# Merging a layer norm with a mixture of experts, and spreading the routing weights by DMA

## The chip, the cores and the metric

The kernel runs on one core of a Trainium2 chip. Its time is the device time of one execution, in microseconds (us). Five engines work side by side and meet at semaphores: TensorE (PE, matrix products into PSUM banks of 128 x 512 float32), VectorE (DVE), ScalarE (ACT), GpSimd (POOL) and SyncE (SP), whose queue issues the transfers here. Everything below is float32 unless a row says bf16.

## The reference, cut to what matters

The input x has 4 sequences of 1024 tokens with 128 features, 4096 tokens in all. Four blocks follow one another, each added to x:

```python
x = x + delta_attention(layernorm(x))
x = x + ffn(layernorm(x))          # first mixture
x = x + decay_attention(layernorm(x))
x = x + ffn(layernorm(x))          # second mixture, same weights
```

The change lies in the two feed-forward mixtures and the plain layer norms before them:

```python
def layernorm(x, eps=1e-05):       # over the 128 features
    m, v = mean(x), var(x)
    return (x - m) / sqrt(v + eps)

def ffn(xt):                       # 15 experts, 3 of them per token
    shared = relu(xt @ sW1 + sb1) @ sW2 + sb2
    probs  = softmax(xt @ router_W + router_b)
    top_p, top_i = top_k(probs, 3)
    cw     = zeros((n, 15)); cw[row, top_i] = top_p
    h      = relu(einsum('nd,edh->neh', xt, eW1) + eb1)   # hidden size 128
    ye     = einsum('neh,ehd->ned', h, eW2) + eb2
    return shared + einsum('ned,ne->nd', ye, cw)
```

Every expert is computed for every token; the routing weight cw is zero for the twelve that were not chosen.

## The kernel before, in words

Activations stay in SBUF transposed: features on the 128 partitions, tokens along the row (g.xT, and g.xn for the normed copy). Work goes in NT = 8 tiles of 512 tokens. The kernel is a row of blocks; between two blocks all engines meet at a barrier and the semaphores of the block are cleared. Inside a block each engine has its own program, written in the order in which it runs, with explicit waits. There is no planner.

**The layer norm** (layernorm, L170 to L263). For each tile TensorE centres the features with a product (L191), ScalarE squares and copies the result (L224, L227), TensorE sums the squares (L198), ScalarE takes the square root (L233), VectorE inverts it (L246), TensorE spreads it over the partitions (L206), and VectorE multiplies (L253). The order of TensorE is variance(i), centre(i + 2), replicate(i - 1).

**The mixture** (mixture, L1248 to L1492). First a block b0 in which POOL raises about 80 semaphores by two (L1290). Then the main block: after a few memsets on VectorE, SP issues eleven loads (L1320), among them both sets of expert weights and a selecting matrix sel, and all engines wait for all of them. VectorE casts sel to bf16 (L1418). Then the routing of tile 0 runs alone: logits (r_lt, L1331 and L1385), their turn to tokens on partitions (r_tr, L1337), maximum and subtraction (r_sub), exponential (L1389), the three largest probabilities (r_top, L1427 to L1449), the turn back (r_ct, L1343), and a split of the weights into three bf16 parts that sum to the float32 value (r_parts, L1451 to L1466).

Then, for each tile, sixteen experts (the shared one is the sixteenth). For expert e TensorE computes the hidden layer ph (L1356) and the product pc that copies row e of the routing weights to all 128 partitions (L1358: sel times the three parts); ScalarE applies relu (L1399); VectorE multiplies by pc (L1478, a plain copy L1480 for the shared expert) into hs; TensorE adds the second layer into py (L1367). ph, pc, hr and hs have two buffers each, and TensorE runs hidden(e + 1) before the second layer of e. The bias product (L1363) opens py. The routing of the next tile is laid between the experts: r_lt behind e = 1, r_tr behind e = 3, r_ct behind e = 10 on TensorE, r_top behind e = 6 and r_parts behind e = 11 on VectorE. At the end of a tile VectorE adds py to x (L1490). The tile loop is a hardware loop over pairs of tiles with two tiles behind it (tiles, L1304).

Of the kernel before, what the change touches and what calls it, by code (L numbers as in the profile page):

```python
# [31 lines left out]
CREDIT = 2  # L32
TILE = 512
# [8 lines left out]


def done(n):

    return n + 1 + CREDIT


def constants():
# [1198 lines left out]
def mixture(nc, g, tag):  # L1248


    NE = E_N + 1
    with ExitStack() as ctx:
        new_sem = semaphores(nc, ctx)
        sb = lambda n, s, dt=F32: ctx.enter_context(nc.sbuf_tensor(tag + n, s, dt))
        pb = lambda n, s: ctx.enter_context(nc.psum_tensor(tag + n, s, F32))
        sem = lambda n: new_sem(tag + n)
        w1, w2 = sb("w1", [128, NE, 128]), sb("w2", [128, NE, 128])
# [6 lines left out]
        mx = sb("mx", [128, 4])  # L1264
        den = sb("den", [128, 4])
        p20 = sb("p20", [128, 4, 20])
        m20 = sb("m20", [128, 4, 20])
# [4 lines left out]
        rest = sb("rest", [NE, 2, TILE])  # L1272
        midw = sb("midw", [NE, TILE], BF16)
        parts = [sb(f"parts{i}", [96, TILE], BF16) for i in range(2)]
        hr, hs = sb("hr", [128, 2, TILE]), sb("hs", [128, 2, TILE])
        ph, pc, py = ([pb(f"{n}{i}", [128, TILE]) for i in range(2)] for n in ("ph", "pc", "py"))
        pl, pt = pb("pl", [128, TILE]), pb("pt", [128, TILE])
        evs = []

        def ev(n):  # L1280
            evs.append(sem(n))
            return evs[-1]

        hc_mm, relu, hs_ev, y_mm = ([ev(f"{n}{e}") for e in range(NE)] for n in ("hc_mm", "relu", "scaled", "y_mm"))
        lt_mm, lt_ev, tr_mm, mx_ev, sub_ev, exp_ev, den_ev, rden_ev, p_ev, top_ev, topf_ev, m_ev, cw_ev, ct_mm, ct_ev = (
            ev(n) for n in ("lt_mm", "lt_ready", "tr_mm", "max_ready", "sub_ready", "exp_ready", "den_ready", "rden_ready", "p_ready",
                            "top_ready", "top3_ready", "match_ready", "cw_ready", "ct_mm", "cwt_ready"))
        hi_ev, r1_ev, mid_ev, r2_ev, parts_ev, acc_ev = (ev(n) for n in ("hi_ready", "r1_ready", "mid_ready", "r2_ready", "parts_ready", "acc_ready"))
        loaded, zeroed, const = sem("loaded"), sem("zeroed"), sem("const")
        with nc.Block() as b0:  # L1290
            @b0.gpsimd
            def _(pool):
                for s in evs:
                    pool.sem_inc(s, CREDIT)
        block = ctx.enter_context(nc.Block())
        d = g.dram
        loads = [(w1[:, 0:E_N, :], d["eW1"].rearrange("e d h -> d e h")), (w1[:, E_N, :], d["sW1"]),
                 (w2[:, 0:E_N, :], d["eW2"].rearrange("e d h -> d e h")), (w2[:, E_N, :], d["sW2"]),
                 (b1[:, 0:E_N], d["eb1"].rearrange("e h -> h e")), (b1[:, E_N:NE], d["sb1"].unsqueeze(1)),
                 (b2[0:E_N, :], d["eb2"]), (b2[E_N:NE, :], d["sb2"].unsqueeze(0)),  # L1300
                 (rw[:, 0:E_N], d["router_W"]), (rb[0:E_N, :], d["router_b"].unsqueeze(1)), (self32[:, :], d["c_sel"])]
        NPAIR = NT // 2

        def tiles(eng, step, lead):  # L1304

            lead(0, 0, 0)
            with eng.Fori(0, NPAIR - 1) as j:
# [511 lines left out]
```

## Time and profile before

| what | us |
|---|---|
| median of three runs (3720.75 to 3724.38) | 3722.41 |
| the profiled execution's own time | 3720.53 |
| its span, first to last instruction | 3718.7 |
| first merged stretch: first centring product of the norm to the end of the mixture's last addition | 2556.59 to 2924.13 |
| second one | 3337.67 to 3705.70 |

Busy shares over the whole span are PE 90%, PEld (weight loads) 68%, DVE 75%, ACT 61% and POOL 56%, but most of the span is the delta attention (up to 2554.96), which has nothing to do with the change. A span is what the instructions cover; the execution's own time adds what lies around it, 1.8 us here. All times of rows are us from the start of the span. A reader should look at the stretches of the norms and mixtures alone. One float32 product over 512 columns shows as two MATMUL records; the durations of overlapping records are modelled, so the distance between the starts tells more than the duration.

### The profile page before, as it was taken

How to read it: one execution, taken by the hardware profiler on the slowest of the kernel's cores; microseconds unless marked ns; L12 is line 12 of the kernel's file. 1: busy time of each engine (PE TensorE's matmuls, PEld its weight loads, DVE VectorE, ACT ScalarE, POOL GpSimd, SP SyncE). 2: the span in 40 equal slices, each digit the busy share in tenths (PEclk: the TensorE clock that was granted, in tenths of full speed). 3: DMA queues.
4: the chain of work that ended last, by engine and by line, in shares of the span. 5: the costliest groups of instructions: out<-in, count | busy, mean ns of one | idle time of the engine just before them, and what ended most of it. 6: DMA issues, size and time to landing. Idle time of an engine off the chain costs nothing. (4 is left out here: it accounts for less than half of the span.)

```text
span 3718.7 us, 84350 instructions
## 1 busy us (share of the span) xinstructions
PE 3337.8 (90%) x27220; PEld 2546.1 (68%) x27220; DVE 2786.4 (75%) x6092; ACT 2254.8 (61%) x6799; POOL 2067.5 (56%) x3164
## 2 busy tenths in 40 slices
PE   5359999999999999999999999996899876795998
PEld 3248888888888888888888888874333456672333
DVE  3469999999999999999999999763444469543443
ACT  3368888888888888888888888742233310002333
POOL 1188888888888888888888888830000027100000
PEclk8679999999999999999999999998899985557999
DMA  2557787788787778778877777632000000001000
GB/s 63 160 132 180 181 180 166 175 188 177 170 182 173 178 179 174 171 171 187 179 170 179 171 174 180 159 95 56 1 0 0 1 10 1 1 1 31 0 0 23
DMA packets 603120, 429.38 MB, mean 115 GB/s; under 512 B 497164, under 2 KB 524332, under 8 KB 602700
## 3 DMA queue, kind: packets, MB, share of 16 engines
q1 hardware_dynamic: 600396, 417.86, 49.4%
q10 hardware_dynamic: 2304, 6.29, 0.6%
q8 instruction: 218, 3.57, 0.5%
q14 instruction: 202, 1.65, 0.2%
HBM read 224.25 MB, written 199.75 MB: 114 GB/s over the span
## 5 line engine op out<-in xcount | busy, mean ns | idle before, releaser
L743 POOL TENSOR_TENSOR X<-X,tmp 96x31 f32<-96x31 f32 (+15 forms) x992 | 534.1, 538 | 77.8
L740 POOL TENSOR_TENSOR tmp<-At,X 96x31 f32<-96x31 f32 (+15 forms) x992 | 482.4, 486 | 118.8 <-DMA At<-n_d 63.6
L1610 POOL TENSOR_TENSOR b_P<-b_P,b_tmp 128x512 f32<-128x512 f32 x80 | 114.4, 1430 | 517.6 <-DVE b_tmp L1628 512.8
L1101 PE MATMUL PP<-xn,wk 128*128 128x268 f32 x1024 | 310.9, 406 | 61.3 <-DMA tk<-in_conv_q_dram 41.0
L708 POOL TENSOR_TENSOR Sg<-S,gend 128x512 f32<-128x512 f32 x256 | 276.4, 1080 | 109.8 <-DVE S L927 109.8
L803 ACT ACTIVATE conv_k<-PP,tk 128x256 f32<-128x256 f32 x512 | 235.9, 471 | 108.0 <-PE PP L1101 102.5
L1065 PE MATMUL RB<-rhs,Yf 96*96 96x128 f32 x2048 | 276.3, 278 | 9.8 <-DVE rhs L916 9.3
L767 ACT ACTIVATE recA<-TG 128x128 f32<-128x128 f32 x1024 | 265.6, 275 | 31.8 <-PE TG L1152 31.8
L1065 PEld LDWEIGHTS RB<-rhs,Yf 96*96 96x96 f32 x2048 | 239.6, 163 | 64.7 <-DVE rhs L916 52.5
L775 ACT ACTIVATE recA<-TG,es 96x128 f32<-96x128 f32 x1024 | 273.7, 368 | 16.2 <-DVE es L951 15.9
L1055 PE MATMUL RA<-S,kqgB 128*96 128x128 f32 x2048 | 275.1, 277 | 0.7 <-DVE S L927 0.7
L1075 PE MATMUL RA<-ws,recB 96*128 96x128 f32 x2048 | 271.5, 276 | 0.7 <-ACT ws L793 0.7
L1055 PEld LDWEIGHTS RA<-S,kqgB 128*96 128x96 f32 x2048 | 240.2, 163 | 39.8 <-issue 25.2
L1075 PEld LDWEIGHTS RA<-ws,recB 96*128 96x128 f32 x2048 | 260.0, 192 | 7.7 <-ACT ws L793 0.9
L965 DVE SCALAR_TENSOR_TENSOR conv_k<-PP,tk,conv_k 128x256 f32<-128x256 f32 x512 | 247.8, 484 | 18.3
L963 DVE SCALAR_TENSOR_TENSOR conv_k<-PP,tk,conv_k 128x256 f32<-128x256 f32 x512 | 247.7, 484 | 18.2
L961 DVE SCALAR_TENSOR_TENSOR conv_k<-PP,tk,conv_k 128x256 f32<-128x256 f32 x512 | 244.2, 477 | 22.2 <-ACT conv_k L803 20.6
L803 ACT ACTIVATE conv_v<-PP,tv 128x256 f32<-128x256 f32 x384 | 183.7, 478 | 126.7 <-PE PP L1101 112.3
L693 POOL TENSOR_TENSOR kqgA<-kq,gdec 128x768 f32<-128x768 f32 x128 | 202.7, 1584 | 80.4 <-ACT kq L844 73.6
L1101 PE MATMUL PP<-xn,wv 128*128 128x268 f32 x768 | 242.1, 396 | 2.1 <-DVE conv_k L965 2.1
L1101 PEld LDWEIGHTS PP<-xn,wk 128*128 128x128 f32 x1024 | 170.8, 197 | 82.2 <-DMA tk<-in_conv_q_dram 41.8
L1164 PE MATMUL TG<-kq 128*96 128x128 f32 x1888 | 225.6, 273 | 0.7 <-ACT recA L775 0.7
(314 smaller groups left out, 8396.6 us busy)
## 6 DMA issues: line engine op xcount, KB each, us to landing
kqg_d<-kqgA SPq DMA_DIRECT2D x128, 512.0 KB, 5.1
kqgB<-kqg_d SPq DMA_DIRECT2D x128, 512.0 KB, 7.3
rec_d<-recA SPq DMA_DIRECT2D x128, 480.0 KB, 3.7
recB<-rec_d SPq DMA_DIRECT2D x128, 480.0 KB, 8.6
gdec<-gdec_d SPq DMA_DIRECT2D x128, 128.0 KB, 6.6
apk_d<-apkA SPq DMA_DIRECT2D x128, 128.0 KB, 2.5
apkB<-apk_d SPq DMA_DIRECT2D x128, 128.0 KB, 6.7
edec<-edec_d SPq DMA_DIRECT2D x128, 96.0 KB, 6.2
```

Of the source, the lines that this page charges most:

```text
L708: nc.gpsimd.tensor_tensor(Sg[:, :, :], S[cc][:, :, :], d.broadcast_to([128, B, 128]), ALU.mult).then_inc(sg_ev[cc], 1)
L740: nc.gpsimd.tensor_tensor(t, At[q % 2][:, j, j + 1:].unsqueeze(2).broadcast_to(sh), X[q % 2][:, j, 0:cols].unsqueeze(1).broadcast_to(sh), ...
L743: nc.gpsimd.tensor_tensor(x, x, t, ALU.subtract).then_inc(sub_ev, 1)
L767: last = nc.scalar.activation(recA[N % 2][:, u * 128:(u + 1) * 128], TG[:, u, :], ACT.Square, accum_out=ksum[:, u:u + 1])
L775: last = nc.scalar.activation(recA[N % 2][0:R, u * 128:(u + 1) * 128], TG[0:R, u, :], ACT.Copy, scale=es[:, u, TC - 1:TC])
L803: nc.scalar.activation(acc, src[:, :, 0:SPAN], ACT.Copy, scale=w).then_inc(tap0_ev[i], 1)
L963: nc.vector.scalar_tensor_tensor(acc, src[:, :, 2:2 + SPAN], w[:, 2:3], acc, ALU.mult, ALU.add).then_inc(t2_ev[i], 1)
L965: nc.vector.scalar_tensor_tensor(acc, src[:, :, 3:3 + SPAN], w[:, 3:4], acc, ALU.mult, ALU.add).then_inc(taps_ev[i], 1)
L1055: last = mm(RA[0:R, b, :], kqgB[N % 2][:, b * NCC + cc, 0:R], S[cc][:, b, :], start=True, stop=True)
L1065: last = mm(RB[0:R, b, :], Yf[N % 2][:, b * NCC + cc, :], rhs[:, b, :], start=True, stop=True)
L1075: last = mm(RA[:, b, :], recB[N % 2][:, u * 128:(u + 1) * 128], ws[cc][:, b, :], start=True, stop=True)
L1101: mm(out, w, x, start=True, stop=True).then_inc(tile_mm[i], 1)
```

## The change

The norm and the mixture behind it become one function and one block, twice. The weights are issued by SP at the block's start, in the order router, first layer, second layer, with a semaphore for each group, while the norm runs. The routing of tile 0 is laid into the norm's loop. The block of POOL increments is gone, and the tile loop is written out. The three bf16 parts, sel and the product pc are gone. In their place VectorE copies the routing weights of a tile to cwt (r_cwt), SP stores the 15 rows of cwt to DRAM, waits for that, and issues four transfers that read 4, 4, 4 and 3 rows back into all 128 partitions (gates, 15 x 512 float32 on each partition, two buffers). VectorE then multiplies hr by gates, both in SBUF. ph, hr and hs have four buffers, TensorE runs hidden(e + 2) before the second layer of e, also over the tile's end, and the addition to x moves behind the second expert of the next tile. In the routing of the next tile r_lt, r_tr and r_ct stand behind e = 0, 2 and 7, and VectorE's r_sub, r_top and r_cwt behind e = 3, 5 and 8. The functions take, root, centre, variance, replicate, invert and norm are those of layernorm; r_sub and r_top are the same instructions as before.

```diff
-    sel = np.zeros((96, E_N, 128), np.float32)
-    for part in range(3):
-        for e in range(E_N):
-            sel[32 * part + e, e] = 1
-    c["c_sel"] = sel.reshape(96, -1)
...
-def mixture(nc, g, tag):
-
+def normed_mixture(nc, g, tag):
 
     NE = E_N + 1
+    QUARTER = TILE // 4
+    DEEP = 4
+    GROUPS = [(0, 4), (4, 8), (8, 12), (12, E_N)]
...
-        self32 = sb("sel32", [96, E_N * 128])
-        sel = sb("sel", [96, E_N, 128], BF16)
+        xc = sb("xc", [128, 4, TILE])
+        sq = sb("sq", [128, 2, TILE])
+        rs = sb("rs", [128, 4, QUARTER])
+        eps = sb("eps", [128, 1])
...
+        gates = [sb(f"gates{i}", [128, E_N, TILE]) for i in range(2)]
+        hr, hs = sb("hr", [128, DEEP, TILE]), sb("hs", [128, DEEP, TILE])
+        gates_d = nc.dram_tensor(tag + "gates_d", (2, E_N, TILE), F32, kind="Internal").ap()
+        ph = [pb(f"ph{i}") for i in range(DEEP)]
+        py = [pb(f"py{i}") for i in range(2)]
+        pl, pt = pb("pl"), pb("pt")
+        cen, var, rep = ph[0:2], ph[2:4], py
...
         @block.sync
         def _(sp):
             sp.wait_ge(zeroed, 1)
...
-            for dst, src in loads:
-                sp.dma_start(dst, src, allow_slow_non_contiguous=True).then_inc(loaded, 16)
+            sp.dma_start(rw[:, 0:E_N], d["router_W"], allow_slow_non_contiguous=True).then_inc(router_in, 16)
+            sp.dma_start(rb[0:E_N, :], d["router_b"].unsqueeze(1), allow_slow_non_contiguous=True).then_inc(router_in, 16)
+            sp.dma_start(w1[:, 0:E_N, :], d["eW1"].rearrange("e d h -> d e h")).then_inc(w1_in, 16)
...
+            for n in range(NT):
+                sp.wait_ge(ct_ev, n + 1)
+                sp.dma_start(gates_d[n % 2], cwt[n % 2][0:E_N, :]).then_inc(gates_out, 16)
+                sp.wait_ge(gates_out, 16 * (n + 1))
+                need(sp, hs_ev[E_N - 1], n - 2)
+                for k, (a, b) in enumerate(GROUPS):
+                    sp.dma_start(gates[n % 2][:, a:b, :], gates_d[n % 2, a:b].partition_broadcast(128)).then_inc(gates_in[n % 2][k], 16)
...
+            def r_lt(n):
+                if n == 0:
+                    pe.wait_ge(router_in, 32)
+                    pe.wait_ge(scaled, 1)
+                need(pe, ct_ev, n - 1)
+                mm(pl[0:NE, :], rw[:, :], xn_of(n), start=True, stop=True).then_inc(lt_mm, 1)
...
+            def hidden(n, e):
+                n, e = n + e // NE, e % NE
+                if n == NT:
+                    return
+                if e >= DEEP:
+                    pe.wait_ge(relu[e - DEEP], n + 1)
+                else:
+                    need(pe, relu[NE + e - DEEP], n - 1)
+                mm(ph[e % DEEP][:, :], w1[:, e, :], xn_of(n), start=True, stop=True).then_inc(h_mm[e], 1)
+
+            centre(0)
+            centre(1)
+            for i in range(NT + 1):
+                if i < NT:
+                    variance(i)
+                if i + 2 < NT:
+                    centre(i + 2)
+                if i:
+                    replicate(i - 1)
+                if i == 2:
+                    r_lt(0)
+                if i == 4:
+                    r_tr(0)
+                if i == 7:
+                    r_ct(0)
+            pe.wait_ge(scaled, NT)
+            pe.wait_ge(copied, NT)
+            pe.wait_ge(rooted, NT)
+            pe.wait_ge(w1_in, 64)
+            hidden(0, 0)
+            hidden(0, 1)
+            pe.wait_ge(w2_in, 64)
+            for n in range(NT):
+                pe.wait_ge(ct_ev, n + 1)
+                need(pe, acc_ev, n - 2)
+                mm(py[n % 2][:, :], b2[:, :], cwt[n % 2][:, :], start=True, stop=False)
                 for e in range(NE):
...
+                    hidden(n, e + 2)
+                    pe.wait_ge(hs_ev[e], n + 1)
+                    mm(py[n % 2][:, :], w2[:, e, :], hs[:, e % DEEP, :], start=False, stop=e == NE - 1).then_inc(y_mm[e], 1)
+                    if n + 1 < NT:
+                        if e == 0:
+                            r_lt(n + 1)
+                        if e == 2:
+                            r_tr(n + 1)
+                        if e == 7:
+                            r_ct(n + 1)
...
+            act.wait_ge(eps_ready, 1)
+            take(0)
+            take(1)
+            for i in range(NT):
+                root(i)
+                if i + 2 < NT:
+                    take(i + 2)
+                if i == 2:
+                    act.wait_ge(router_in, 32)
+                    r_lt(0)
+                if i == 5:
+                    r_exp(0)
+            act.wait_ge(w1_in, 64)
+            for n in range(NT):
                 for e in range(NE):
-                    act.wait_ge(hc_mm[e], done(n))
-                    act.wait_ge(hs_ev[e - 2], done(n) if e >= 2 else done(n - 1))
-                    nc.scalar.activation(hr[:, e % 2, :], ph[e % 2][:, :], ACT.Relu, bias=b1[:, e:e + 1]).then_inc(relu[e], 1)
-                    if n1 is not None:
+                    act.wait_ge(h_mm[e], n + 1)
+                    if e >= DEEP:
+                        act.wait_ge(hs_ev[e - DEEP], n + 1)
+                    else:
+                        need(act, hs_ev[NE + e - DEEP], n - 1)
+                    nc.scalar.activation(hr[:, e % DEEP, :], ph[e % DEEP][:, :], ACT.Relu, bias=b1[:, e:e + 1]).then_inc(relu[e], 1)
+                    if n + 1 < NT:
                         if e == 2:
-                            r_lt(n1)
-                        if e == 5:
-                            r_exp(n1)
-
-            tiles(act, step, lead)
+                            r_lt(n + 1)
+                        if e == 4:
+                            r_exp(n + 1)
...
+            def r_cwt(n):
+                dve.wait_ge(ct_mm, n + 1)
+                need(dve, y_mm[0], n - 2)
+                if n >= 2:
+                    dve.wait_ge(gates_out, 16 * (n - 1))
+                nc.vector.tensor_copy(cwt[n % 2][:, :], pl[0:NE, :]).then_inc(ct_ev, 1)
...
+            invert(0)
+            for i in range(NT):
+                if i + 1 < NT:
+                    invert(i + 1)
+                norm(i)
+                if i == 3:
+                    r_sub(0)
+                if i == 5:
+                    r_top(0)
+            def add(n):
+                dve.wait_ge(y_mm[NE - 1], n + 1)
+                nc.vector.tensor_tensor(x_of(n), py[n % 2][:, :], x_of(n), ALU.add).then_inc(acc_ev, 1)
+
+            r_cwt(0)
+            for n in range(NT):
                 for e in range(NE):
-                    dve.wait_ge(relu[e], done(n))
-                    dve.wait_ge(y_mm[e - 2], done(n) if e >= 2 else done(n - 1))
+                    if n and e == 2:
+                        add(n - 1)
+                    dve.wait_ge(relu[e], n + 1)
+                    if e >= DEEP:
+                        dve.wait_ge(y_mm[e - DEEP], n + 1)
+                    else:
+                        need(dve, y_mm[NE + e - DEEP], n - 1)
                     if e < E_N:
-                        nc.vector.tensor_tensor(hs[:, e % 2, :], pc[e % 2][:, :], hr[:, e % 2, :], ALU.mult).then_inc(hs_ev[e], 1)
+                        if e % 4 == 0:
+                            dve.wait_ge(gates_in[n % 2][e // 4], 16 * (n // 2 + 1))
+                        nc.vector.tensor_tensor(hs[:, e % DEEP, :], gates[n % 2][:, e, :], hr[:, e % DEEP, :], ALU.mult).then_inc(hs_ev[e], 1)
                     else:
-                        nc.vector.tensor_copy(hs[:, e % 2, :], hr[:, e % 2, :]).then_inc(hs_ev[e], 1)
-                    if n1 is not None:
-                        if e == 4:
-                            r_sub(n1)
-                        if e == 6:
-                            r_top(n1)
-                        if e == 11:
-                            r_parts(n1, 1 - par)
-                dve.wait_ge(y_mm[NE - 1], done(n))
-                x = g.xT[:, bass.ds(j, 1), TILE * par:TILE * (par + 1)]
-                nc.vector.tensor_tensor(x, py[par][:, :].unsqueeze(1), x, ALU.add).then_inc(acc_ev, 1)
-
-            tiles(dve, step, lead)
+                        nc.vector.tensor_copy(hs[:, e % DEEP, :], hr[:, e % DEEP, :]).then_inc(hs_ev[e], 1)
+                    if n + 1 < NT:
+                        if e == 3:
+                            r_sub(n + 1)
+                        if e == 5:
+                            r_top(n + 1)
+                        if e == 8:
+                            r_cwt(n + 1)
+            add(NT - 1)
...
-        layernorm(nc, g, "ln1", x_tile)
-        mixture(nc, g, "f1")
+        normed_mixture(nc, g, "f1")
...
-        layernorm(nc, g, "ln4", x_tile)
-        mixture(nc, g, "f2")
+        normed_mixture(nc, g, "f2")
```

## Rows read from the trace of the kernel before

**Rows 1.** Busy time by engine in both mixtures: us, PE, PEld, DVE, ACT, POOL, PEclk, DMA, GB/s

```profile
2618.65:2924.13 305.48, 287.24 (x746) 117.69 (x746) 132.77 (x332) 93.67 (x142) 0.00 (x0) 0.98 0.00 0
3400.24:3705.70 305.46, 287.23 (x746) 117.82 (x746) 132.77 (x332) 93.67 (x142) 0.00 (x0) 0.98 0.00 0
```

**Rows 2.** Groups of instructions, first mixture: busy, mean ns | idle before, releasers

```profile
L1367 PE MATMUL f1py<-f1hs,f1w 128*128 128x512 f32 x256 | 134.4, 606 | 17.5 <-DVE f1hs L1478 14.9 <-DVE f1hs L1480 2.6
...
L1478 DVE TENSOR_TENSOR f1hs<-f1pc,f1hr 128x512 f32<-128x512 f32 x120 | 82.3, 691 | 148.3 <-ACT f1hr L1399 148.0
```

**Rows 3.** Timeline of one undisturbed expert: start, us, engine, line, op, count

```profile
2910.33 1.02 PE L1356 MATMUL f1ph<-xn,f1w 128*128 128x512 f32 x2
...
2911.19 0.38 PE L1358 MATMUL f1pc<-f1parts,f1sel 96*128 96x512 bf16 x1
...
2911.41 1.02 PE L1367 MATMUL f1py<-f1hs,f1w 128*128 128x512 f32 x2
...
2912.27 1.02 PE L1356 MATMUL f1ph<-xn,f1w 128*128 128x512 f32 x2
```

**Rows 4.** Timeline of one whole tile, from fifteenth expert to fifteenth expert

```profile
2735.80 1.07 PE L1367 MATMUL f1py<-f1hs,f1w 128*128 128x512 f32 x2
...
2744.46 1.03 PE L1331 MATMUL f1pl<-xn,f1rw 128*16 x2
...
2749.49 1.06 PE L1337 MATMUL f1pt<-ident,f1lt 16*128 16x16 f32 x8
...
2750.48 1.12 PE L1356 MATMUL f1ph<-xn,f1w 128*128 x2
...
2764.82 0.60 PE L1343 MATMUL f1pl<-ident,f1cw 128*16 128x128 f32 x4
...
2773.91 1.07 PE L1367 MATMUL f1py<-f1hs,f1w 128*128 128x512 f32 x2
```

**Rows 5.** Timeline of norm, lead-in and end of the first mixture

```profile
2556.59 3.75 PE L191 MATMUL ln1cen<-xT,centre 128*128 128x512 f32 x4 [2.08 <-PEq L91]
...
2579.01 0.69 DVE L253 TENSOR_TENSOR xn<-ln1rep,ln1xc 128x512 f32<-128x512 f32 x1 [0.70 <-PE ln1rep L206]
...
2604.35 1.16 DVE L1418 CAST f1sel<-f1sel 96x1920 bf16<-96x1920 f32 x1 [16.12 <-DMA f1sel<-in_c_sel_dram]
...
2625.38 1.92 PE L1367 MATMUL f1py<-f1hs,f1w 128*128 128x512 f32 x2
...
2923.44 0.69 DVE L1490 TENSOR_TENSOR xT<-f1py,xT 128x512 f32<-128x512 f32 x1 [1.22 <-PE f1py L1367]
```

**Rows 6.** Timeline of VectorE, first and last instruction of r_top

```profile
2755.13 0.20 DVE L1429 TENSOR_REDUCE f1den<-f1lg 128x4 f32<-128x60 f32 x1
...
2757.17 0.22 DVE L1449 SCALAR_TENSOR_TENSOR f1cw<-f1m,f1p 128x60 f32<-128x60 f32 x1
```

**Rows 7.** Timeline of ScalarE in the norm, table load and square root

```profile
2561.48 1.28 ACT L233 ACT_TABLE_LOAD   x1
...
2562.77 0.37 ACT L233 ACTIVATE ln1rs<-ln1var,ln1eps 128x128 f32<-128x128 f32 x1
```

**Rows 8.** DMA issues of the whole span: KB each, median us to landing

```profile
gdec<-gdec_d SPq DMA_DIRECT2D x128, 128.0 KB, 6.6
...
apkB<-apk_d SPq DMA_DIRECT2D x128, 128.0 KB, 6.7
...
n_d<-apkA SPq DMA_DIRECT2D x384, 32.0 KB, 2.2
...
xin<-in_x_dram SPq DMA_DIRECT2D x4, 512.0 KB, 4.0
```

**Rows 9.** Busy time by engine: the loads at their densest, and the delta attention

```profile
2592.00:2594.00 2.00, 0.00 (x0) 0.00 (x0) 0.00 (x0) 0.00 (x0) 0.00 (x0) 0.50 1.17 297
...
600.00:700.00 100.00, 99.84 (x1007) 85.84 (x1006) 94.54 (x215) 85.58 (x280) 85.00 (x135) 1.00 0.83 188
```

**Rows 10.** Busy time by engine: TensorE's clock as it rises, norm and mixture

```profile
2561.00:2562.00 1.00, 1.00 (x7) 0.24 (x9) 0.00 (x0) 0.98 (x2) 0.00 (x0) 1.00 0.00 0
...
2628.00:2630.00 2.00, 2.00 (x5) 0.57 (x3) 0.00 (x0) 0.69 (x1) 0.00 (x0) 0.76 0.00 0
```

More of the change, by code:

```diff
@@ L1295, in mixture @@
+        zeroed, router_in, w1_in, w2_in, gates_out = (sem(n) for n in ("zeroed", "router_in", "w1_in", "w2_in", "gates_out"))
+        gates_in = [[sem(f"gates_in{p}_{k}") for k in range(len(GROUPS))] for p in range(2)]
         block = ctx.enter_context(nc.Block())
         d = g.dram
[L1297 to L1307, printed above, removed]
-                step(j * 2, j, 0, j * 2 + 1, j)
-                step(j * 2 + 1, j, 1, j * 2 + 2, j + 1)
-            step(NT - 2, NPAIR - 1, 0, NT - 1, NPAIR - 1)
-            step(NT - 1, NPAIR - 1, 1, None, None)
-        def xn(j, par):
-            return g.xn[:, bass.ds(j, 1), PAD + TILE * par:PAD + TILE * (par + 1)]
+        x_of = lambda i: g.xT[:, i // 2, TILE * (i % 2):TILE * (i % 2 + 1)]
@@ L1340, in r_ct @@
             def r_ct(n):
[L1341 removed]
+                pe.wait_ge(cw_ev, n + 1)
                 for a in range(4):
@@ L1376, in _ @@
-            tiles(pe, step, lead)
+            def hidden(n, e):
[22 more added lines that the diff above has]
+                    r_ct(0)
@@ L1378, in _, with take, root @@
         @block.scalar
         def _(act):
-            act.wait_ge(loaded, 16 * len(loads))
+            def take(i):
+                act.wait_ge(centred, i + 1)
+                need(act, varied, i - 2)
+                nc.scalar.activation(sq[:, i % 2, :], cen[i % 2][:, :], ACT.Square).then_inc(squared, 1)
+                need(act, scaled, i - 4)
+                nc.scalar.activation(xc[:, i % 4, :], cen[i % 2][:, :], ACT.Copy).then_inc(copied, 1)
+            def root(i):
+                act.wait_ge(varied, i + 1)
+                need(act, spread, i - 4)
+                nc.scalar.activation(rs[:, i % 4, :], var[i % 2][:, 0:QUARTER], ACT.Sqrt, bias=eps[:, :]).then_inc(rooted, 1)
@@ L1451, in r_parts @@
-            def r_parts(n, par):
-                dve.wait_ge(ct_mm, done(n))
-                dve.wait_ge(y_mm[NE - 1], done(n - 2))
-                hi, mid, lo = (parts[par][32 * i:32 * i + NE, :] for i in range(3))
-                nc.vector.tensor_copy(cwt[par][:, :], pl[0:NE, :]).then_inc(ct_ev, 1)
-                nc.vector.tensor_copy(hi, pl[0:NE, :]).then_inc(hi_ev, 1)
-                dve.wait_ge(hi_ev, done(n))
-                nc.vector.tensor_tensor(rest[:, 0, :], pl[0:NE, :], hi, ALU.subtract).then_inc(r1_ev, 1)
-                dve.wait_ge(r1_ev, done(n))
-                nc.vector.tensor_copy(midw[:, :], rest[:, 0, :]).then_inc(mid_ev, 1)
-                dve.wait_ge(mid_ev, done(n))
-                nc.vector.tensor_copy(mid, midw[:, :])
-                nc.vector.tensor_tensor(rest[:, 1, :], rest[:, 0, :], midw[:, :], ALU.subtract).then_inc(r2_ev, 1)
-                dve.wait_ge(r2_ev, done(n))
-                nc.vector.tensor_copy(lo, rest[:, 1, :]).then_inc(parts_ev, 1)
@@ L1468, in lead @@
-            def lead(n, j, par):
-                r_sub(n)
-                r_top(n)
-                r_parts(n, par)
-            def step(n, j, par, n1, j1):
-                for e in range(NE):
-                    dve.wait_ge(relu[e], done(n))
-                    dve.wait_ge(y_mm[e - 2], done(n) if e >= 2 else done(n - 1))
+            invert(0)
[7 more added lines that the diff above has]
+                    r_top(0)
```

180 lines of the change are left out of this document (75 added, 105 removed).

## The prediction

> **What bounds the kernel now.** I read the busy time by stage first. Each mixture's main part lasts 305.5 us with TensorE busy 287, VectorE 133, ScalarE 94 and no DMA [rows 1]. So TensorE sets the pace there, and the DMA engines are free. The groups by line then say what TensorE still waits for: 17.5 us of idle time before the second-layer product L1367, released by VectorE [rows 2].
>
> The timeline of one expert gives the price list: hidden product 0.86 us (start to start, less the copy product), copy product 0.22, second layer 0.86, together 1.94 [rows 3]. Any float32 product over 512 columns costs 0.86. A whole tile takes 2773.91 - 2735.80 = 38.1 us [rows 4]. Its work is 15 x 1.94 + 1.72 = 30.8 for the experts, 0.86 for the bias product, 0.86 for the logits, 0.99 for r_tr (2749.49 to 2750.48) and 0.60 for r_ct, in all 34.1. The other 4.0 us are waits: two buffers leave little room when VectorE is away for r_top (2755.13 to 2757.39 = 2.26 us [rows 6]) or for the seven instructions of r_parts.
>
> The timeline of the lead-in shows the second cost. The norm ends at 2579.01 + 0.69 = 2579.70, VectorE gets its last load and casts sel at 2604.35 after waiting 16.1 us for transfers, and the first second-layer product starts at 2625.38 [rows 5]. From the block's start to that product pass 68.8 us, of which the norm is 23.1.
>
> **The change, part by part.** Times are for one mixture; the second has the same main part to 0.02 us [rows 1], and I take it as equal.
>
> *Norm with the routing of tile 0 inside.* TensorE gets r_lt and r_tr before the norm's end, 0.86 + 0.99 = 1.85, and is fully busy there [rows 10]. ScalarE must change tables for the exponential between two square roots and back: two loads of 1.28 [rows 7] and the small exponential, 2.8. VectorE has r_top, 2.26, in front of invert(7), and the norm's tail is a chain through all three engines. The three add up to 6.9 if nothing overlaps. Bounds: 3 (all but the table change hidden) and 9. I take 6.9, since the tail is serial: the norm ends at +30.0.
>
> A rule of the Trainium skill speaks against this step (ScalarE: Activation LUTs, What ACT_TABLE_LOAD costs): a switch costs the load and a drain of about 1.38 us more. In rows 7 the square root starts 1.29 us after its load does, so this trace shows no drain; by the rule the two switches would add 2.8 us a mixture, and the forecast would be 5.5 us later.
>
> *Loads.* Their wait (16.1 us, rows 5) lies under a norm of 30 us; without c_sel there is less of it. SP issues nothing else then. Cost nothing; if the cover were gone, at most the few us by which they end later than the norm.
>
> *From the norm's end to the first expert.* r_cwt is one copy, 0.7. The store is 30 KB; the nearest row has 32 KB landing in 2.2 [rows 8]. SP waits for it and issues the four broadcasts; behind that wait on SP stand only these. The first moves 128 x 8 KB = 960 KB. The nearest plain load is 512 KB in 4.0 [rows 8]; the other 448 KB at 297 GB/s [rows 9] make 1.5, together 5.5. From below the pure rate bounds it, 983,040 bytes at 297 = 3.3; from above the only broadcast in the trace, 128 KB in 6.6 among other traffic [rows 8], and the rest at 188 GB/s [rows 9], 11.1. Then one multiplication, 0.7, and hand-overs of 0.2: 30.0 + 0.7 + 2.2 + 5.5 + 0.9 = +39.3. Before it was +68.8, so 29.5 us go. By then three hidden products and the bias product are done.
>
> *The tile.* No pc: 15 x 0.22 = 3.3 us less. The waits: between the end of hidden(e) and the second layer of e now lie four products, 3.4 us. Relu 0.69, multiplication 0.69 [rows 2] and three hand-overs take about 1.7. VectorE's r_top behind e = 5 takes 2.26; the next multiplication ends 2.26 + 0.69 = 2.95 after the last, and is due 1.7 + 1.72 = 3.4 after it: hidden. r_cwt is short. At the tile's end the hidden products run on. So all 4.0 us go; bounds 0 and 4.0. What is late next is TensorE itself: 32 x 0.86 + 0.86 + 0.86 + 0.99 + 0.60 = 30.8 with routing, 28.4 in the last tile. VectorE has about 16 us of work in it. The multiplication from two SBUF operands has no row; it could take up to 2.4 us (0.69 + the 1.7 of room) without being seen.
>
> *The gates of the next tile.* From r_ct to the next tile's first second layer TensorE has 18 products, 15.5 us; less cwt 0.9 and one multiplication 0.7, 13.9 remain for store and first broadcast, 7.7. The other groups come every 3.3 us and are used up in 4 x 1.72 = 6.9. All four are 3.93 MB: 13.2 us at 297 GB/s, 20.9 at 188, both under 30.8. Hidden. Uncovered, the tile would last as long as its transfers; that begins under 128 GB/s. TensorE and VectorE lose nothing to traffic by rows 9: TensorE is 99.84% busy at full clock beside 188 GB/s.
>
> *The clock.* TensorE stands idle for some us before the first gates and starts at 1.2 GHz (0.50). In the norm the full clock (1.00) is there 4 to 5 us after the first product, in the mixture it comes about 11 us after 2618.65 [rows 1, 10]. Half speed over 7 us, between them, loses 3.5; bounds 0 and 5.5.
>
> *The sum.* From the first second layer: 7 x 30.8 + 28.4 - 4 x 0.86 = 240.6, + 3.5 for the clock, + 0.9 for the last addition = 245.0. Before: 2924.13 - 2625.38 = 298.8. So 53.8 + 29.5 = 83.3 a mixture, 166.5 in both. The profiled execution took 3720.53: 3554.0. It lies 1.9 under the median shown, so 3556.
>
> **The rivals.**
>
> *A: stalls stay.* Waits move to the gates' semaphores or to VectorE. For: VectorE waits in order and r_top is within 0.5 us of the limit. Against: 1.7 us of room each expert. If all 4.0 stay in 16 tiles: 3556 + 64 = 3620.
>
> *B: the broadcasts set the pace, but the kernel is still faster.* 128 partitions read the same 8 KB at once, from few places in DRAM. Against: the broadcast in rows 8 lands as fast as a plain load of its size, 6.6 against 6.7. For: that is an eighth of the size and bound by latency. At 110 GB/s the tile is 35.7: + 4.9 x 16 = 78, 3634; anywhere from 3560 to 3715.
>
> *C: slower than before.* The same mechanism below a threshold: the saving of 166 us is eaten when a tile takes 166 / 16 = 10.4 us more, 41.2, that is below 95 GB/s. Its form: a transfer that runs on a quarter of the 16 DMA engines, 297 / 4 = 74 GB/s, tile 53, + 22 x 16 = 355: 3910. For: groups have four rows. Against: rows 8, and every load onto 128 partitions in rows 9 runs near 300.
>
> The Trainium skill (DMA: Bandwidth & Descriptors, Rules for kernel authors) has the rule behind C: the slowest dimension of both sides sets how many engines a DMA uses, so a leading broadcast of few copies confines it to as many. Here the leading dimension is the 128 partitions, which by the rule uses all 16; no run here shows it for this shape yet.
>
> *D: the change doesn't do what it says.* The loads might not end under the norm: they took 16 us alone, and now start with it. Then the lead-in keeps up to 10 us, + 20: 3576. The trace gives nothing for that.
>
> **How the numbers follow.** Forecast 0.76, A 0.09, B 0.08, C 0.05, D 0.02. The forecast's own range adds its bounds: from -(3.9 norm, 2.2 first gates, 3.5 clock) x 2 = -19 to +(2.1 + 5.6 + 2.0) x 2 = +19, 3537 to 3575. Up to 3620 it takes in A, D and part of B: 3535 to 3620, with about 2 in 10 outside, most of it below my trust in the small terms. About 0.2% (7 us) is what a measurement of this kernel can tell from no change. Faster 0.94, same 0.01 (B or C close to 95 GB/s), slower 0.05.
>
> **What would show it.** Right: no MATMUL from sel; starts of second-layer products 1.72 apart, r_top included; tiles of 30.8 with TensorE busy throughout; first second layer about 39 us after the first centring product, with 7 to 8 us of TensorE idle before it released by a DMA; transfers done 13 to 21 us after their issue in each tile. Wrong: VectorE waiting for gates in tiles 1 to 7 (B, C), idle time on TensorE behind r_top (A), ScalarE or TensorE waiting for w1 or w2 (D). A norm that ends before +27 or after +33 would make my 6.9 wrong.

## The result, and the profile after

The changed kernel takes 3561.21 us (median of 4 runs, 3555.57 to 3564.35), the kernel before beside it 3722.22: a ratio of 0.9566, 95% interval 0.9552 to 0.9581. The forecast was 3556, in a range of 3535 to 3620. In a second set of 5 runs (a1_after) it took 3558.09 against 3722.92, ratio 0.9558 [0.9545, 0.9571]; the experiments below are compared with this one. "Ratio" is the time over that of the kernel before in the same set, with its 95% interval.

The profiled execution took 3555.57, its span is 3553.5. The two merged stretches, busy time by engine, from the first centring product to the end of the last addition (columns as in [rows 1]):

```profile
2560.36:2847.12 286.76, 280.41 (x784) 122.83 (x784) 126.36 (x333) 111.63 (x172) 0.00 (x0) 0.96 0.31 118
3253.46:3540.01 286.55, 280.29 (x784) 123.03 (x784) 126.36 (x333) 111.63 (x172) 0.00 (x0) 0.96 0.31 119
```

TensorE is busy for 280.4 of 286.8 us. Before, the same stretch lasted 2924.13 - 2556.59 = 367.5 us [rows 5], so 80.8 us went here and about 81 in the second, 162 of the 165 between the two profiled runs. I had forecast 284.3 and 83.3.

The groups that answer to [rows 2], from the first second-layer product on:

```profile
L1386 PE MATMUL f1py<-f1hs,f1w 128*128 128x512 f32 x256 | 131.3, 595 | 0.0
L1355 PE MATMUL f1ph<-xn,f1w 128*128 128x512 f32 x251 | 131.0, 603 | 0.0
L1526 DVE TENSOR_TENSOR f1hs<-f1gates,f1hr 128x512 f32<-128x512 f32 x119 | 81.8, 690 | 100.7 <-ACT f1hr L1438 100.7
L1386 PEld LDWEIGHTS f1py<-f1hs,f1w 128*128 128x128 f32 x256 | 48.5, 190 | 62.4 <-issue 60.5 <-DVE f1hs L1526 1.4 <-DVE f1hs L1528 0.4
```

The 17.5 us in front of the second-layer product are 0.0 now, and from here on VectorE's multiplication waits for ScalarE's relu alone, never for gates. The last row is the weight load that belongs to the product, on an engine row of its own (PEld): its 1.4 us behind VectorE are idle time of the loads, not of the products. TensorE's timeline over one tile, from bias product to bias product (answers to [rows 4]):

```profile
2723.87 1.02 PE L1386 MATMUL f1py<-f1hs,f1w 128*128 128x512 f32 x2
2724.82 1.12 PE L1382 MATMUL f1py<-f1cwt,f1b 16*128 16x512 f32 x2
2725.87 1.13 PE L1355 MATMUL f1ph<-xn,f1w 128*128 128x512 f32 x2
2726.83 1.02 PE L1386 MATMUL f1py<-f1hs,f1w 128*128 128x512 f32 x2
2727.78 1.03 PE L1332 MATMUL f1pl<-xn,f1rw 128*16 128x512 f32 x2
2728.75 1.12 PE L1355 MATMUL f1ph<-xn,f1w 128*128 128x512 f32 x2
2729.71 1.02 PE L1386 MATMUL f1py<-f1hs,f1w 128*128 128x512 f32 x2
2730.57 1.02 PE L1355 MATMUL f1ph<-xn,f1w 128*128 128x512 f32 x2
2731.43 1.02 PE L1386 MATMUL f1py<-f1hs,f1w 128*128 128x512 f32 x2
...
2756.32 1.12 PE L1382 MATMUL f1py<-f1cwt,f1b 16*128 16x512 f32 x2
```

Second layers stand 2731.43 - 2729.71 = 1.72 apart, as forecast, but the tile is 2756.32 - 2724.82 = 31.50, not 30.8: around the bias product, the logits and r_tr, whose shapes differ, the starts stand 0.95 to 1.05 apart and not 0.86. TensorE waits for nothing; these 0.7 us are its own.

The norm's end and the lead-in, which answer to [rows 5]:

```profile
2580.47 1.28 ACT L1416 ACT_TABLE_LOAD   x1
2581.76 0.25 ACT L1416 ACTIVATE f1lg<-f1lg 128x60 f32<-128x60 f32 x1
2582.03 1.28 ACT L1407 ACT_TABLE_LOAD   x1
2583.33 0.62 ACT L1407 ACTIVATE f1rs<-f1ph,f1eps 128x128 f32<-128x128 f32 x2
2583.73 0.95 DVE L1449 RECIPROCAL f1rs<-f1rs 128x128 f32<-128x128 f32 x1 [2.78 <-ACT f1rs L1407]
...
2590.43 0.69 DVE L1454 TENSOR_TENSOR xn<-f1py,f1xc 128x512 f32<-128x512 f32 x1 [1.62 <-PE f1py L1324]
...
2591.73 0.32 SPq L1299 DMA_DIRECT2D f1gates_d<-f1cwt  x1
...
2593.26 2.03 SPq L1303 DMA_DIRECT2D f1gates<-f1gates_d  x4
...
2596.89 2.08 PE L1355 MATMUL f1ph<-xn,f1w 128*128 128x512 f32 x2
...
2598.06 1.29 DVE L1526 TENSOR_TENSOR f1hs<-f1gates,f1hr 128x512 f32<-128x512 f32 x2 [6.36 <-DMA f1gates<-f1gates_d]
...
2598.81 2.08 PE L1386 MATMUL f1py<-f1hs,f1w 128*128 128x512 f32 x2
```

The norm ends at 2591.12, +30.8 from the start (a time with a plus sign counts from the merged stretch's first centring product); the first second-layer product stands at +38.4, in the second mixture too. Broadcasts, as a DMA group of the page and by busy time (the last three columns are the granted clock, the DMA share and GB/s):

```profile
f1gates<-f1gates_d SPq DMA_DIRECT2D x24, 1024.0 KB, 6.6
```

```profile
2595.00:2597.00 2.00, 2.00 (x3) 0.50 (x3) 0.00 (x0) 0.68 (x1) 0.00 (x0) 0.50 1.03 426
2601.00:2603.00 2.00, 2.00 (x3) 0.37 (x2) 0.00 (x0) 0.26 (x1) 0.00 (x0) 0.54 0.97 410
2603.00:2605.00 2.00, 2.00 (x6) 0.80 (x6) 0.40 (x1) 1.10 (x2) 0.00 (x0) 1.00 0.57 229
2632.00:2847.00 215.00, 214.39 (x540) 91.94 (x538) 94.83 (x249) 81.19 (x122) 0.00 (x0) 1.00 0.27 111
```

They keep all 16 DMA engines busy (shares of 0.97 to 1.03) at 410 to 426 GB/s, over the 297 of [rows 9]; in the tiles they fill 27% of the time.

### The profile page after: what moved, and what is told of

Read it like the earlier page. It is cut to its first block and busy times, and to the rows that moved or that the text cites. A ratio compares the mean times of both kernels' runs of the same rounds, so it can differ in the third digit from the quotient of the medians.

```text
span 3553.5 us, 83210 instructions
## 1 busy us (share of the span) xinstructions
PE 3264.9 (92%) x26980; PEld 2519.4 (71%) x26980; DVE 2732.4 (77%) x5990; ACT 2264.8 (64%) x6803; POOL 2070.6 (58%) x3164
## 5 line engine op out<-in xcount | busy, mean ns | idle before, releaser
L1054 PEld LDWEIGHTS RB<-rhs,Yf 96*96 96x96 f32 x2048 | 239.5, 162 | 64.8 <-DVE rhs L905 52.5
L952 DVE SCALAR_TENSOR_TENSOR conv_k<-PP,tk,conv_k 128x256 f32<-128x256 f32 x512 | 247.8, 484 | 18.2
```

The lines of the kernel that those rows point to most:

```text
L952: nc.vector.scalar_tensor_tensor(acc, src[:, :, 2:2 + SPAN], w[:, 2:3], acc, ALU.mult, ALU.add).then_inc(t2_ev[i], 1)
L1054: last = mm(RB[0:R, b, :], Yf[N % 2][:, b * NCC + cc, :], rhs[:, b, :], start=True, stop=True)
```

## The experiments

**The whole change, and the merging alone.** a1_after is the changed kernel again.

> The changed kernel again, for its spread and for a second profile. If the changed parts are steady and the 9 us between its runs come from elsewhere (theory: TensorE's clock in the two attentions, which the change does not touch), both merged stretches last 286 to 287 us again, first centring product to last addition, and the rest of the span differs by several us from the first profile. If the spread comes from the broadcasts (rival), the merged stretches differ by several us between the profiles and VectorE waits for gates in some tile after the first.

Measured: 3558.09 (above). The theory holds: the merged stretches last 286.0 and 286.6 us, and the time between them is 9.6 us longer than in the first profile (415.9 for 406.3), in parts that the change does not touch. a2_merge merges norm and mixture and loads under the norm, but keeps the copy product with r_parts, the two buffers (the ring of two) and the old order in the tile:

Its edit against the changed kernel, the core of it:

```
-    DEEP = 4
+    DEEP = 2
...
+            sp.dma_start(self32[:, :], d["c_sel"]).then_inc(sel_in, 16)
...
-                    sp.dma_start(gates[n % 2][:, a:b, :], gates_d[n % 2, a:b].partition_broadcast(128)).then_inc(gates_in[n % 2][k], 16)
...
+                        last = mm(pc[e % 2][:, :], sel[:, e, :], parts[n % 2][:, :], start=True, stop=True)
...
-                    hidden(n, e + 2)
+                    hidden(n, e + 1)
...
-                        if e == 7:
+                        if e == 10:
                             r_ct(n + 1)
...
+                nc.vector.tensor_copy(hi, pl[0:NE, :]).then_inc(hi_ev, 1)
```

> Only the merging: norm and mixture in one block, loads under the norm, routing of tile 0 in the norm, no block of POOL increments, tile loop written out; but the copy product from three bf16 parts, two buffers, hidden(e + 1) and the old places of the routing stay. Theory: the first second-layer product comes at +43 us instead of +68.8 (norm to +30.8, seven instructions of r_parts 4.3, cast 1.2, five cold products 6.7) and the tiles stay at 38.1, so 3722 - 2 x 26 = 3670. Rival, that writing the loop out or the moved addition matters too: below 3655.

Measured: 3673.93 (3672.14 to 3675.03), ratio 0.9870 [0.9854, 0.9885]. First second-layer product at +42.7, tiles of 38.11 as before. Merging is worth 49 us, all of it ahead of the first expert: from the first second-layer product on, the two mixtures last 299.0 and 298.7 us, in the kernel before 298.8 and 298.7.

**The ring.** a3_ring2 is the changed kernel with two buffers instead of four:

```
-    DEEP = 4
+    DEEP = 2
...
-        cen, var, rep = ph[0:2], ph[2:4], py
+        var = [pb(f"var{i}") for i in range(2)]
+        cen, rep = ph, py
...
             hidden(0, 0)
-            hidden(0, 1)
...
-                    hidden(n, e + 2)
+                    hidden(n, e + 1)
```

> The changed kernel with rings of two for ph, hr and hs and hidden(e + 1) ahead of the second layer; gates by DMA as in the change. Between the end of hidden(e) and the second layer of e stand two products, 1.72 us, against 1.66 for relu, multiplication and hand-overs. Theory, the ring hides what VectorE does between: r_top 2.3, cwt 0.7, the addition 0.7 and the subtraction 0.5 come out on TensorE, about 4 us a tile, + 64: 3625. Rival, the waits of before came from the copy product and r_parts, which are gone anyway: within 15 us of the changed kernel, 3575.

Measured: 3582.65 (3573.93 to 3586.73), ratio 0.9623 [0.9603, 0.9644]; tiles of 32.85. My theory was wrong, the rival (3575) nearly right. TensorE in one tile of this kernel, around r_top:

```profile
2740.89 1.02 PE L1356 MATMUL f1ph<-xn,f1w 128*128 128x512 f32 x2
2742.72 1.13 PE L1386 MATMUL f1py<-f1hs,f1w 128*128 128x512 f32 x2 [0.80 <-DVE f1hs L1526]
2743.68 1.02 PE L1356 MATMUL f1ph<-xn,f1w 128*128 128x512 f32 x2
```

One wait a tile, 0.80 us with 0.17 of start-up, and nothing of the rest, but for slips of 0.05. The kernel before had three, of which two end here (lines of its timeline, same columns):

```profile
2757.25 0.38 PE L1358 MATMUL f1pc<-f1parts,f1sel 96*128 96x512 bf16 x1
2758.04 1.13 PE L1367 MATMUL f1py<-f1hs,f1w 128*128 128x512 f32 x2 [0.41 <-DVE f1hs L1478]
...
2768.05 0.38 PE L1358 MATMUL f1pc<-f1parts,f1sel 96*128 96x512 bf16 x1
2770.15 1.13 PE L1367 MATMUL f1py<-f1hs,f1w 128*128 128x512 f32 x2 [1.72 <-DVE f1hs L1478]
...
2775.31 1.13 PE L1367 MATMUL f1py<-f1hs,f1w 128*128 128x512 f32 x2 [0.33 <-DVE f1hs L1480]
```

0.22 is the undisturbed distance, so 0.57 is lost behind r_top and 1.88 behind r_parts. At the last expert 0.54 more is lost: its second layer starts at 2775.31, 1.40 behind the one at 2773.91 [rows 4], where 0.86 is undisturbed. The largest was r_parts, which went with the copy product, without a deeper ring.

So the gain is made up of 49.0 for merging, 3673.9 - 3582.7 = 91.3 for gates by DMA, and 3582.7 - 3558.1 = 24.6 for the ring; by the mixtures' own lengths in the traces it is 52.5, 86.0 and 23.8. The middle part is not the gates alone. a3_ring2 differs from a2_merge in the order of the tile too: the routing of the next tile stands earlier, the addition is moved, and the hidden products run on over the tile's end. The 0.54 us at the last expert went with that order, in 16 tiles about 9 us (an estimate). No run has four buffers together with the copy product, so what the ring alone would have given the old kernel stays open.

**The threshold of rival B.** a4_four issues three spare copies beside each broadcast, into tiles that nobody reads: 15.73 MB a tile instead of 3.93.

```
                     sp.dma_start(gates[n % 2][:, a:b, :], gates_d[n % 2, a:b].partition_broadcast(128)).then_inc(gates_in[n % 2][k], 16)
+                    for x in range(3):
+                        need(sp, spare_in[x], 16 * (4 * n + k) - 1)
+                        sp.dma_start(spare[x][:, 0:b - a, :], gates_d[n % 2, a:b].partition_broadcast(128)).then_inc(spare_in[x], 16)
```

> The changed kernel, but every broadcast is followed by three more of the same rows into spare buffers that nobody reads, so 15.7 MB a tile instead of 3.93. If the rate of 425 GB/s that the profile shows in one tile holds, a tile's transfers take 37.0 us and with the store between them about 40, more than TensorE's 30.8: tiles of 40, + 9.2 x 14 = + 129, about 3690, and VectorE waits for gates. If the rate falls under sustained load to the 297 that I had assumed, tiles of 55 and about 3900. If transfers cost TensorE or VectorE time of their own, products and multiplications show longer durations.

Measured: 3704.63 (3703.15 to 3707.73), ratio 0.9952 [0.9936, 0.9968]. Busy time over six tiles (the last three columns are again the granted clock, the DMA share and GB/s), and VectorE's group in them:

```profile
2640.00:2880.00 240.00, 207.57 (x482) 83.42 (x480) 81.44 (x234) 71.57 (x108) 0.00 (x0) 0.94 0.95 391
```

```profile
L1533 DVE TENSOR_TENSOR f1hs<-f1gates,f1hr 128x512 f32<-128x512 f32 x90 | 59.1, 686 | 131.0 <-DMA f1gates<-f1gates_d 103.7 <-ACT f1hr L1445 27.3
```

The wait in front of the multiplication is a DMA's now, as rival B has it. The tiles take 39.98 on average (bias products at 2639.43 and 2879.29, six tiles), and 15.73 MB in that are 393 GB/s. It takes four times the traffic to bring the kernel back near its old time, and even then VectorE's multiplication lasts 686 ns beside it, not more than the 690 of the changed kernel. The mixtures last 355.5 and 359.9, together 142.0 more than the changed kernel's. My 129 counted 14 tiles. From the first bias product to the last, 14 tiles of the two mixtures, 118.7 us were added; the two last tiles, from the bias product to the end of the last addition, take 38.8 and 40.1 us instead of 27.8, 23.3 more. They wait for their gates too, and I had left them out: most of the 14.6 us over my 3690.

**Loads not hidden (rival D).** c_late holds the weight loads until the norm is done:

```
             sp.dma_start(rb[0:E_N, :], d["router_b"].unsqueeze(1), allow_slow_non_contiguous=True).then_inc(router_in, 16)
+            sp.wait_ge(scaled, NT)
             sp.dma_start(w1[:, 0:E_N, :], d["eW1"].rearrange("e d h -> d e h")).then_inc(w1_in, 16)
```

> The changed kernel with the mixture's weight loads held back until the norm's last product. Theory: placing them under the norm is worth what they take behind it: SP needs about 9.6 us to issue them and the last lands 6 us later, so the store of the gates comes 9 to 10 us later and the first second-layer product at about +50 instead of +38.5: 3558 + 23 = 3581. Rival: the routing and the gates' trip would have covered most of it anyway: 3558 + 6 = 3564.

Measured: 3579.34 (3573.91 to 3582.82), ratio 0.9611 [0.9596, 0.9627]; first second-layer product at +48.0 and +47.8, each mixture 296.8, 10.1 more. In the timeline of SP's queue the store of the gates stands behind the eight issues:

```profile
2588.24 0.41 SPq L1290 DMA_DIRECT2D f1w<-in_eW_dram  x1
...
2590.49 3.32 SPq L1293 DMA_DIRECT2D f1b<-in_sb_dram  x1
...
2596.67 0.32 SPq L1300 DMA_DIRECT2D f1gates_d<-f1cwt  x1
...
2600.21 1.96 SPq L1304 DMA_DIRECT2D f1gates<-f1gates_d  x4
```

The delay is first SP's issuing, 2596.67 - 2588.24 = 8.4 us, then a store that takes 3.5 instead of 1.5 us to come back. In the changed kernel, where the loads start is worth 21 us in all. That it is also 21 of the 49 us of merging is not shown: a2_merge was not run with late loads.

**The norm's tail.** b1_exp_late moves tile 0's exponential behind the last root, so that no table is loaded back:

```
-                if i == 7:
+                if i == NT:
                     r_ct(0)
...
-                if i == 5:
-                    r_exp(0)
+            r_exp(0)
...
-                if i == 5:
+                if i == 6:
                     r_top(0)
```

> The changed kernel with the exponential of tile 0 behind the last square root, r_top(0) behind the seventh norm product and r_ct(0) behind the last replication. Theory: the norm's tail waits for the two table loads (VectorE idle 2.8 us before the seventh reciprocal) and with the exponential last, one of the two leaves the path and r_top fills another engine's time: the norm ends 4 us earlier (at +26.5 to +27), the first second-layer product at +34.5; 3558 - 8 = 3550. Rival: the tail is set by the router's own chain (exponential, r_top, r_ct, cwt) wherever it stands: within 2 us of 3558.

Measured: 3552.71 (3547.24 to 3565.22), ratio 0.9552 [0.9534, 0.9570]. The times overlap with those of a1_after, the traces decide: the norm ends at +26.6 in both mixtures (before the move +30.8), the first second-layer product is at +34.2 and +34.4, the mixtures last 282.8 and 283.0. The theory holds: the reload and r_top in front of the last reciprocal, moved together here, cost 4.2 us of the tail; no run parts the two.

b2_small_first splits off the first gate row:

```
-    GROUPS = [(0, 4), (4, 8), (8, 12), (12, E_N)]
+    GROUPS = [(0, 1), (1, 4), (4, 8), (8, 12), (12, E_N)]
```

> The changed kernel with broadcasts of 1, 3, 4, 4 and 3 gate rows instead of 4, 4, 4 and 3. Theory: the first multiplication waits for 1 MB at about 420 GB/s, and would be released some 1.9 us earlier by a quarter of it; TensorE, which waits for the gates for only 1.4 us, gains 1 us a mixture at most: 3556. Rival: the landing is latency, not bytes, and nothing changes: 3558. In the tiles neither sees a difference, since the gates are there early.

Measured: 3560.17 (3544.96 to 3562.74), ratio 0.9565 [0.9551, 0.9578]: medians cannot tell 2 us here. The first multiplication starts at +36.8 in both mixtures, 0.4 to 0.9 us earlier than in the two profiles of the changed kernel, not 1.9. A first group of 256 KB lands 3.8 us after its issue, one of 1024 KB after 4.2 to 4.7, so the landing is mostly latency. But this run's two mixtures, the same instructions, lasted 283.9 and 286.5. Busy time at about equal distance from their starts (+34.7 and +35.0):

```profile
2589.00:2591.00 2.00, 2.00 (x4) 0.48 (x4) 0.00 (x0) 0.64 (x1) 0.00 (x0) 1.00 0.83 301
```

```profile
3278.00:3280.00 2.00, 2.00 (x3) 0.50 (x3) 0.18 (x1) 0.35 (x1) 0.00 (x0) 0.50 0.98 340
```

The granted clock (third number from the end) is 1.00 in the one and 0.50 in the other: the full clock came back before the first second-layer product in one and behind it in the other. That product moved to +37.5 in the first and stayed at +38.4 in the second. What set its time in the second was TensorE at half clock, not the gates; my expectation, that TensorE waits 1.4 us for them, had read the idle time of the weight loads.

b3_warm gives TensorE spare products in the norm's last waits:

```
+            def spare(k):
+                for _ in range(k):
+                    mm(pt[:, :], g.centre[:, :], x_of(0), start=True, stop=True)
...
+                if i == 7:
+                    pe.wait_ge(sub_ev, 1)
+                    spare(3)
                 if i:
                     replicate(i - 1)
...
                 if i == 7:
+                    spare(2)
                     r_ct(0)
```

> The changed kernel with five spare products (0.43 to 0.6 us each, into a tile that is free then) on TensorE in its idle time at the norm's end, three before replicate(6) and two before r_ct(0). Theory: the idle time there is what drops the granted clock to 0.50 until about 10 us later, and the cold clock costs 0.5 us in r_ct, 0.9 in the last replication, 1.9 behind the first second-layer product: kept busy, the norm ends about 1 us earlier and the rest runs at full clock, 3558 - 6 = 3552, the granted clock 1.00 at the first hidden product. Rival: the clock falls all the same in the wait for the gates, or rises too late: within 1 us of 3558.

Measured: 3558.22 (3555.11 to 3562.64), ratio 0.9559 [0.9546, 0.9572]. The norm ends 1.0 us earlier (+29.7 and +29.8), its clock stays at 1.00, and then falls while TensorE waits 3.3 us for the gates (3.7 in the second mixture): the cold stretch was moved, not removed. The mixtures last 285.2 and 286.4.

```profile
2592.00:2594.00 2.00, 1.33 (x3) 0.30 (x2) 0.00 (x0) 0.63 (x1) 0.00 (x0) 1.00 0.90 303
...
2598.00:2600.00 2.00, 2.00 (x3) 0.13 (x2) 0.00 (x0) 0.00 (x0) 0.00 (x0) 0.50 0.98 414
```

**Together.** b4_both is b1_exp_late with b2_small_first; b5_best adds spare products in front of the first second layer, b6_three takes three of them instead of five:

```
                     hidden(n, e + 2)
+                    if n == 0 and e == 0:
+                        for _ in range(5):
+                            mm(pt[:, :], g.centre[:, :], xn_of(0), start=True, stop=True)
                     pe.wait_ge(hs_ev[e], n + 1)
```

> The same without the spare products. Theory: the clock falls in the 4 us in which TensorE waits for the gates, and costs about 2 us behind them: each mixture about 281.5 to 282, 3549. Rival: with the first gates 1.5 us earlier the clock stays at 1.00 by itself: 280.0, 3545.5.

> The changed kernel with the exponential, r_top and r_ct of tile 0 at the end of the norm, broadcasts of 1, 3, 4, 4 and 3 rows, and five spare products on TensorE in its wait for the first gates. Theory: norm end at +26.5, first second-layer product at +32.5 to +33 (1.5 us less by the small first group), and the spare products keep the granted clock at 1.00, which saves 1.9 us more: each mixture about 280.0 instead of 286.3, 3558 - 12.5 = 3545.5. Rival: the clock drops anyway and the rest only shifts the wait to the second group of gates: each mixture at 282.5, 3550. The attention between the mixtures moves by some 5 us either way by its own clock, so the mixtures' own times decide.

> The last but one kernel with three spare products instead of five. A spare product of 128x512 takes 0.86 us, not the 0.43 of one of its two records, so that five (4.3 us) overran the wait of 3.1 us; three (2.6) fit. Theory: the clock stays at 1.00 and nothing is delayed: first second-layer product at +33.6, 246.4 us behind it, each mixture 280.0 to 280.5 against 282.6 without spare products, 3547. Rival: the idle 0.5 us that is left, or the norm's own tail, drops the clock all the same: 282.5 as without them.

Measured: b4_both 3550.99 (3546.29 to 3552.41), ratio 0.9540 [0.9527, 0.9553], mixtures 282.8 and 282.5, the clock falls in the wait. b5_best 3549.93 (3547.84 to 3554.07), ratio 0.9538 [0.9525, 0.9551]: I had priced a product of two records as one, the five ran into the path (first second layer at +36.3 and +34.8), and 282.6 and 281.1 came out. b6_three 3546.77 (3544.93 to 3557.31), ratio 0.9537 [0.9522, 0.9553], mixtures 280.8 and 279.9, of which 246.3 and 246.4 lie behind the start of the first second layer. Its TensorE:

```profile
2592.22 1.13 PE L1355 MATMUL f1ph<-xn,f1w 128*128 128x512 f32 x2
2593.18 2.74 PE L1387 MATMUL f1pt<-xn,centre 128*128 128x512 f32 x6
2595.76 1.02 PE L1389 MATMUL f1py<-f1hs,f1w 128*128 128x512 f32 x2
```

No gap, and the first second layer lasts 1.02, not the 2.08 of half clock. Against b4_both the ranges overlap, so the stretch behind the first second layer decides, which spare products do not lengthen: 246.3 or 246.4 in all four mixtures of b5_best and b6_three. In the fourteen mixtures with four buffers and no spare products in this wait (a4_four left out) it is 247.8 to 249.1, but for one: 246.4 in the first mixture of b2_small_first. By the mixtures' own times b6_three is 572.6 - 560.7 = 11.9 us faster than a1_after, by medians 11.3.

## Why the prediction was right

*Norm.* Forecast +30.0, measured +30.8: 7.6 us over the 23.1 of before, not 6.9. Compared product by product with the norm before, 1.9 come by r_lt and r_tr, 2.7 by the table change (VectorE idle 2.78), 2.1 by r_top, as forecast, and 0.9 by half clock in the last replication, a term that the prediction did not have. By the rule of the Trainium skill (ScalarE: Activation LUTs, What ACT_TABLE_LOAD costs) each switch would have drained for 1.38 us more. The trace disagrees: 2580.47 + 1.28 = 2581.75 and the exponential starts at 2581.76.

*Loads.* Hidden, as costed; c_late shows 21 us if they were not, as D had it (20).

*First gates.* Forecast 9.3 from norm's end to the first product, measured 2598.81 - 2591.12 = 7.7: the store came back in 1.5 instead of 2.2 and the first broadcast landed in 4.7 (4.2 in the second mixture) instead of 5.5. The 5.5 was itself too small by its own working: 128 x 8 KB are 1024 KB, as the row of the broadcasts says, and not 960, which makes 5.8. The product stood at +38.4 against +39.3. But I expected 7 to 8 us of idle TensorE there, where my own terms left 9.3 - 4 x 0.86 = 5.9, and there was none: the hidden and bias products at half clock filled it. In the first mixture the gates and TensorE's own products are ready together. In the second the first multiplication is done at 3290.69 + 0.69 = 3291.38, and the second layer still starts 1.86 behind the hidden product, the half-clock distance:

```profile
3289.99 2.08 PE L1355 MATMUL f2ph<-xn,f2w 128*128 128x512 f32 x2
3290.69 1.29 DVE L1526 TENSOR_TENSOR f2hs<-f2gates,f2hr 128x512 f32<-128x512 f32 x2 [5.89 <-DMA f2gates<-f2gates_d]
...
3291.85 1.92 PE L1386 MATMUL f2py<-f2hs,f2w 128*128 128x512 f32 x2
```

So 0.4 to 0.5 us of the cold clock are on the path there, and most of its cost shows behind it. In the first mixture of a1_after, with the full clock for the bias product, TensorE does wait 1.51 us for the gates.

*The tile.* Here is the step that was off: "The other 4.0 us are waits", and so "all 4.0 us go". The waits were 0.57 + 0.54 + 1.88 = 3.0, and a start-up of 0.1 behind each; the other 0.7 was TensorE's own, changing to products of other shapes and back, and stayed. Tile 31.50 for 30.8, 7 x 0.70 = 4.9 us a mixture. And "two buffers leave little room" was the smaller part: the ring gave 1.35 of the 6.6 us a tile, the copy product (3.3), r_parts and the order at the tile's end the rest.

*The gates of the next tile.* Hidden: VectorE waits for no DMA in tiles 1 to 7. I had 297 GB/s; it is 406 to 438. What lies beyond the threshold is as I put it (a4_four: tile as long as its transfers); at what rate it begins, my 128 GB/s, was not run. The rule of the Trainium skill (DMA: Bandwidth & Descriptors, Rules for kernel authors) that the slowest dimension sets how many DMA engines a transfer uses spoke against rival C for this shape, and the trace agrees: a DMA share of 1.03, all 16. A form with the rows outermost was not run, so C itself stays untested.

*The clock.* Forecast 3.5 us behind the first product, measured 248.3 - 246.4 (b6_three, whose clock is full there) = 1.9. This term was nearly twice too large, within its bounds of 0 and 5.5.

*Sum.* 284.3 - 0.9 + 4.9 - 1.6 = 286.7 against 286.8. Outside the mixtures the first attention took 3.8 us more than before the change and the second 7.2 less, which the change does not explain: a1_after, the same kernel, took 415.9 us between its mixtures where the first profile took 406.3 and the kernel before 413.5. Busy time in the same 60 us of the decay attention, first run and second:

```profile
3133.00:3193.00 60.00, 57.65 (x301) 48.51 (x302) 31.57 (x82) 2.39 (x4) 0.00 (x0) 0.61 0.00 1
```

```profile
3138.90:3198.90 60.00, 57.65 (x257) 48.71 (x257) 26.81 (x69) 1.79 (x3) 0.00 (x0) 0.53 0.00 1
```

TensorE is equally busy, gets through 301 or 257 products, and the clock is 0.61 or 0.53. So the mechanism was right, but the nearness of 3556 to 3558 and 3561 owes something to small errors of opposite sign (4.9 us too little a mixture in the tiles, 2.5 too much in the lead-in and the clock) and to luck in these stretches; what sets that clock's course stays open.

## What to carry to other kernels

A selecting product that only spreads a row over partitions, with the casts that feed it, can cost more than a trip through DRAM, if the trip starts a good part of a tile ahead and the DMA engines are free: here 91 us, the new order of the tile included, for 3.93 MB a tile. Before crediting a deeper ring, list the waits one by one in a tile's timeline and ask which instruction ends each: most of ours went with the instruction, not with the buffers. Idle time of the weight loads is not idle time of the products: ask the product's own row. Where medians differ by less than what other stages vary, compare the changed stage's own start and end in the traces.

## What the runs showed of the hardware

- A broadcast of 8 KB to 128 partitions runs at 406 to 438 GB/s in stretches of 2 us (after), and four times the traffic at 391 over 240 us (a4_four), faster than the plain loads of [rows 9] at 297. The first 256 KB land 3.8 us after their issue (b2_small_first), the first 1024 KB 4.2 to 4.7 us (after, a1_after).
- VectorE's multiplication of 512 columns takes 690 ns with both operands in SBUF (after), and took 691 with one in PSUM [rows 2].
- Where float32 products change to another shape (16 rows or columns of weights) or back, the start-to-start time is 0.95 to 1.05 us instead of 0.86 (after).
- With the same instructions the granted clock can be 0.50 in one mixture and 1.00 in the next (b2_small_first); 2.6 us of spare products in the last wait kept it at 1.00 through that wait, in both mixtures (b6_three).
